# Moving the wait for the weight stores from the first evacuation of Q to the first write of the attention output

## The reference

```python
qkv = x @ W_attn + b_attn                       # 16 heads of 64
att = softmax(causal(q @ k.T / 8))
x = layernorm(x + (att @ v) @ W_proj + b_proj)
W_real = unfold(G1_R, G2_R)                     # 512 x 512, a tensor-train product
W_imag = unfold(G1_I, G2_I)
re, im = split(x)
f = concat(re @ W_real.T - im @ W_imag.T + b_real,
           re @ W_imag.T + im @ W_real.T + b_imag)
x = layernorm(x + f)
```

## Time and profile before

| | us |
|---|---|
| median of the runs | 1409.7 (1408.85 to 1410.56) |
| the profiled execution | 1411.23 |
| its span on the slowest core (core 3) | 1409.7 |
| spans of the eight cores | 1398.2 to 1409.7 |
| busy on core 3: TensorE, ScalarE, VectorE | 1130.4, 710.3, 509.3 |

### The profile page before, as it was taken

The page is one execution under the profiler, slowest core; times in us unless marked ns, Lnnn a source line. Parts: engine busy times, 40 slices in busy tenths (PEclk is TensorE's granted clock), DMA queues, the critical chain, the costliest instruction groups (busy, mean ns, idle before and its releaser), DMA issues.

```text
span 1409.7 us, 23508 instructions; the slowest of 8 cores (1398.2 to 1409.7 us)
## 1 busy us (share of the span) xinstructions
PE 1130.4 (80%) x8930; PEld 542.1 (38%) x8930; DVE 509.3 (36%) x1015; ACT 710.3 (50%) x842; POOL 114.8 (8%) x137
## 2 busy tenths in 40 slices
PE   2159788887887887798996998788788888789896
PEld 1135333433333433444334543333333333444332
DVE  1145232223223222265573532322322322146475
ACT  1010057766866878456110017687677677835411
POOL 2001100000000000022231000000000000003222
PEclk9999898989899896899998999899899898699898
DMA  7966400000001005150235300000000000443022
GB/s 211 254 100 117 41 6 17 1 17 16 2 15 24 24 1 98 62 178 1 90 125 171 93 1 1 16 16 2 16 17 1 16 17 1 91 125 115 1 120 120
DMA packets 99957, 82.41 MB, mean 58 GB/s; under 512 B 84864, under 2 KB 85000, under 8 KB 98824
## 3 DMA queue, kind: packets, MB, share of 16 engines
q1 hardware_dynamic: 87448, 30.45, 9.5%
q0 software_dynamic: 10912, 37.76, 9.0%
q10 hardware_dynamic: 1488, 12.69, 2.8%
HBM read 52.59 MB, written 24.12 MB: 54 GB/s over the span
## 4 chain that ended last, share of the span: by engine, by line
PE 42%; ACT 18%; DMA 16%; issue 12%; DVE 11%; DVEq 0%; POOL 0%; ACTq 0%; SPq 0%; POOLq 0%
ACT p L567 16%; PE ps_g L466 13%; PE ps_big L547 8%; PE ps_y L619 7%; DMA w2r_d<-w2big 6%; PE ps_big L792 5%; DMA x_tok<-x_in 4%; PE ps_big L400 4%; DMA w2i_d<-w2big 4%; DVE x_tok L808 3%; DVE stats_sb L815 2%; DMA g_sb<-g2i 2%; DVE qp L482 2%; DVE stats_sb L819 1%; PE ps_y L466 1%
## 5 line engine op out<-in xcount | busy, mean ns | idle before, releaser
L567 ACT ACTIVATE p<-ps_big,consts 128x1024 bf16<-128x1024 f32 (+3 forms) x640 | 592.0, 986 | 397.9 <-PE ps_big L547 393.6
L547 PE MATMUL ps_big<-qp,kp 64*128 64x512 bf16 (+3 forms) x1280 | 237.2, 390 | 97.4 <-ACT p L567 94.1
L466 PE MATMUL ps_g<-x_feat,W_sb 128*128 128x512 bf16 x960 | 264.3, 404 | 40.2 <-DVE qp L482 21.2
L583 DVE TENSOR_TENSOR pd<-p,mask_sb 128x256 bf16<-128x256 bf16 x256 | 74.5, 291 | 366.8 <-ACT p L567 275.7
L619 PE MATMUL ps_y<-v_all,p 128*128 128x65 bf16 x3840 | 194.1, 203 | 6.7 <-ACT p L567 6.6
L619 PEld LDWEIGHTS ps_y<-v_all,p 128*128 128x128 bf16 x3840 | 150.1, 103 | 83.8 <-issue 74.8
L547 PEld LDWEIGHTS ps_big<-qp,kp 64*128 64x128 bf16 x1280 | 66.2, 95 | 279.7 <-issue 269.0
L466 PEld LDWEIGHTS ps_g<-x_feat,W_sb 128*128 128x128 bf16 x960 | 83.0, 102 | 114.3 <-issue 60.9
L829 ACT ACTIVATE mv_sb<-mv_sb,consts 128x1 f32<-128x1 f32 x64 | 18.8, 294 | 208.9 <-DVE mv_sb L823 208.9
L792 PE MATMUL ps_big<-Wbig_sb,x_feat 128*128 128x512 bf16 x512 | 120.4, 390 | 0.0
L792 PE MATMUL ps_big<-Wp_sb,x_feat 128*128 128x512 bf16 x512 | 119.4, 388 | 1.0 <-DVE x_feat L735 1.0
(11 more groups left out here) (67 smaller groups left out, 648.8 us busy)
## 6 DMA issues: line engine op xcount, KB each, us to landing
xstage<-x_in POOLq DMA_DIRECT2D x32, 512.0 KB, 5.4
x_tok<-x_in POOLq DMA_DIRECT2D x8, 2048.0 KB, 9.5
out<-x_tok SPq DMA_DIRECT2D x32, 512.0 KB, 2.7
wstage<-w_attn ACTq DMA_DIRECT2D x8, 1536.0 KB, 16.0
ystage_d<-yst SPq DMA_DIRECT2D x12, 512.0 KB, 3.8
Wp_sb<-w_proj POOLq DMA_DIRECT2D x8, 256.0 KB, 9.4
Wbig_sb<-w2r_d POOLq DMA_DIRECT2D x8, 128.0 KB, 2.6
w2r_d<-w2big SPq DMA_DIRECT2D x8, 64.0 KB
```

The costliest lines, as they stand in the source:

```text
L466: return t.matmul(bank[:], W_sb[:, cc * 3072 + j0:cc * 3072 + j0 + 128], x_feat[:, cc * T + tg * 512:cc * T + (tg + 1) * 512], start=(cc = ...
L547: return t.matmul(ps_big[:, off:off + ln], kpb[e * 64:(e + 1) * 64, kk * 128:(kk + 1) * 128], qpb[e * 64:(e + 1) * 64, pos:pos + ln], star ...
L567: return a.activation(o, i, AF.Exp, bias=consts[:, 0:1], scale=0.125)
L583: return v.tensor_tensor(po_, pp, mm_, ALU.mult)
```

## The change

It does two things. w2pad grows from 2,048 to 8,832 float32 per partition, which moves w2big to 94,720 bytes into the region, exactly over ystage0 and ystage1. And the waits for q_w2 and q_w3 are taken from L482 and put at the write of ystage, L664 (in the changed kernel two lines higher, L662).

```diff
-    st_w.enter_context(nc.sbuf_tensor("w2pad", [128, 2048], F32))
+    st_w.enter_context(nc.sbuf_tensor("w2pad", [128, 8832], F32))
...
                             vdv = S.emit("dv", evq,
                                          waits=[("pe", vpe), ("ac", v_bqk),
-                                                ("q_w2", v_w2done),
-                                                ("q_w3", v_w3done),
                                                 G["qk%d" % par]], inc="dv")
...
                             vdv = S.emit("dv", tt_,
-                                         waits=[("dv", vr1), G["yst%d" % par]],
+                                         waits=[("dv", vr1), G["yst%d" % par],
+                                                ("q_w2", v_w2done),
+                                                ("q_w3", v_w3done)],
                                          inc="dv")
```

## The result

The changed kernel takes 1398.9 us in the median against 1408.9 for the kernel before, measured beside it; the ratio is 0.9931 with a 95% interval of 0.9918 to 0.9945, so between 7.8 and 11.6 us less. That is under 1%, but clear of noise. In it the mean of the eight cores' spans was 1392.5 us over six runs of the changed kernel (1390.9 to 1393.9) and 1403.7 over eight of the kernel before (1402.0 to 1406.8): 11.2 us less, and the two don't overlap.

The account below looks back on a forecast made before the run. The prediction took core 3, held by the w2big stores at the first L482, as the bound: -9.83 - 1.81 + 0.7 = -10.9 us, profiled 1411.23 to 1400.3, median 1398.8 us; forecast 1396 to 1401 (0.66), range 1391 to 1405.

Parts of the forecast that it names:

- Term 1: First L482 of sequence 1 on core 3: its idling for the w2big stores goes, -9.83 us.
- Term 2: First to eighth L482 on core 3: without the pause TensorE does not restart at the lower clock, -1.81 us.
- the ruler of sequence 2: Sequence 2 runs the same instructions with nothing to wait for: 1.73 us to first L482, 12.09 to the eighth.
- Term 3: Wait at first L664: due at 183.03, stores in at 169.65, 13.4 us to spare, so no cost.
- Term 4: Eighth L482 to first L664: lower clock after a dense stretch costs 0 to 1.5 us, taken as 0.7.
- Clock below 1.00 in several key blocks: Listed sign that the forecast is wrong: granted clock under full in the first attention key blocks.
- Term 5: Stores from w2big's new address: no slowdown, taken as 0; bounds nothing to 19 us later, 5.6 counting.
- The rest moves as one piece: After the early stretch, later transfers are released by TensorE or engines behind it, so everything shifts by the -10.9 us sum.
- core 3 stays last: End of the kernel: core 3 still ends last, core 5 at about 1394 us.
- that draw for a rival: Slowest core drawn anew to the end: about 1393 us, chance 0.13, or gain eaten, 1408 us, chance 0.06.

Follow-up runs that it names:

- single chain before: The kernel before with its sixteen w2big stores made one chain instead of two, only one store under way; ratio 1.0143 to the kernel before.
- single chain changed: The changed kernel with its sixteen w2big stores made one chain instead of two; ratio 1.0007 to the kernel before.
- versions of the start: The changed kernel with early identity load; with one store chain and split wait; with all these; with early identity, split wait, two held-back chains: 0.9859, 0.9904, 0.9873, 0.9884.
- identity first: The changed kernel with the identity matrix load moved to the front of ScalarE's queue; ratio 0.9859 to the kernel before, 0.9881 when repeated.
- split wait: The changed kernel with one store chain, pair 0's first L662 waiting only for the first eight stores; ratio 0.9904 to the kernel before.

## Why the prediction was right, step by step

Predicted 1398.8, measured 1398.9; such closeness is partly luck, as the interval of the ratio is 3.8 us wide. The gain was forecast as 10.9 us and measured as 9.7 by the ratio, and the kernel before came out 0.8 us lower than in the two runs that the forecast started from. What stands is the mechanism, term by term.

- Term 1, the wait at the first L482: predicted -9.83 on core 3. From v_all to L482 core 3 went from 11.56 to 1.80 us, -9.76; the mean of the cores from 12.3 to 1.8. The kernel with the new address and the old wait kept the idling, 11.5 us from v_all to L482. Shown.
- Term 2, the slow restart: predicted -1.81. Core 3 went from 13.90 to 12.01, -1.89; the mean from 13.8 to 12.0. That this is a price of the pause and not of the stretch: without a pause the stretch takes 12.0 us on every core, and with the wait at the fifth L482 the cores with the longer pauses paid it while the others did not. The Trainium skill (TensorE: Matmul & The Clock Gate, section What's actually happening) says that the ramp costs under 1% of a typical span, and by that the term would have been left out. The trace agrees in size, 1.8 of 1409 us, but it is a seventh of what this change gains in the early stretch, and the ruler of sequence 2 gave it to a tenth of a microsecond.
- Term 3, nothing at the new place: L662 follows its reciprocal on every core, with 0.24 us between. Its margin was 184.28 - 168.88 = 15.4 us on core 3, predicted 13.4. A little is paid. In the kernel before the gap was 0.10, and it is still 0.10 to 0.11 in sequence 2 of the changed kernel, where the waits are left out because the engine has had them. On the cores at full clock the stretch from the eighth L482 to the first write of ystage takes 11.15 instead of 11.02 us. So two waits that are already fulfilled cost 0.13 us here. The wait for bqk at the first L482 looks alike: 1.80 us from v_all in sequence 1, and 1.73 in sequence 2, which has had that wait. That is the 0.07 us by which term 1 fell short, though no run takes this wait away.
- Term 4, the clock in the first key blocks: taken as 0.7, between 0 and 1.5. The mean is 1.1, of which 0.13 belongs to term 3; core 3 paid 1.6. Six of the eight cores had the fall, with a granted clock of 0.72 to 0.91 in the window of 170 to 176 us; the other two kept 1.00 and needed 11.15. "Clock below 1.00 in several key blocks" was one of the prediction's signs of being wrong, and it came. So the size was low by a few tenths, but the range held.
- Term 5, transfers: the last store is in at 167.9 against 168.6, and with the new address alone at 168.2. Shown.
- The rest moves as one piece. The mean first ystage store is 11.3 us earlier, the mean span 10.6. From store to end the cores take 1170.2 us in the mean in the kernel before and 1170.9 in the changed one. The experiments on the wait follow the same line. Against the kernel before, the first store of the profiled execution and the mean of the cores over the runs moved by -7.2 and -8.7 us with the wait at the fifth L482, by +23.0 and +21.9 with the single chain before, and by +0.3 and +0.4 with the single chain changed. In the versions of the start the end followed less well: against the changed kernel -5.4 and -4.7 us with the identity first, -3.0 and -0.6 with the split wait.

The step that failed is "core 3 stays last". Core 3 ended at 1393.2 and core 7 at 1401.5. In nine other runs of the changed kernel the last core is 3, 0, 6, 2, 4, 2, 6, 5 and 5, with the mean of the cores between 1391.7 and 1393.2 and the last core between 1394.9 and 1400.1. So core 3's lag was a draw of that execution, and the time is a draw of eight around a steady mean. The prediction held that draw for a rival; it happens in every run, and the difference of two medians over many runs shows little of it. The sum ought to have been made on the mean of the cores: -10.5 - 1.8 + 1.1 + 0.4 (between the first write of ystage and the first store) - 0.5 (an earlier v_all) = -11.3 at the store.

## What to carry to other kernels

A wait for a shared buffer belongs to the first instruction that truly overwrites it, so choose the overlap of freed memory by who writes last, not by what fits first. When a wait is moved, work out its new margin in time (here 12 to 15 us on the eight cores) and look at what would be held up behind it: the single chain of stores gave back the whole gain at the new place. A second pass through the same code without the wait is the best ruler for what the wait costs, its restart at a lower clock included.

## What was not expected of the hardware

A fall of the clock after a dense stretch is a matter of which core and run: without a pause before the first key blocks, 22 of 40 cores in five kernels (the changed one and the four versions of its start) needed more than 11.5 us from the eighth L482 to the first write of ystage, the others 11.14 to 11.16 (in the second measurements of two of them 9 of 16). With a pause at the first L482, 4 of 24 did (the kernel before, the one with the new address, the single chain before). Sequence 2 of these same three executions has no pause at that place, and there 13 of the 24 needed more than 11.5 us. So the later fall was rarer where a pause came first, and removing the pause gave some of the gain back. Why that is so stays open; no run was made for it.

A load of 64 KB on ScalarE's queue took 6.0 us beside two chains of stores in short runs on SyncE's queue and 2.2 us beside one. The Trainium skill (DMA: Bandwidth & Descriptors, section Queues, rings and completion order) says that a DMA engine takes its queues in turn, a packet at a time. That the load is slowed at all by stores on the other queue agrees with it; but both chains are on one queue, so the rule alone doesn't say why two cost so much more than one, and no run here shows a single engine's turns.
